# A graph network's attention loop: GpSimd forms half of the weighted rows, and three VectorE operations read one operand from PSUM

## What is computed

```
for r in range(8):
    h = x @ W[r]                                  # 3125 x 64
    e = leaky_relu((h @ a_src[r])[src] + (h @ a_dst[r])[dst])   # one number per edge
    e = where(edge_type == r or self loop, e, -inf)
    m = segment_max(e, dst)                       # per target node
    w = exp(e - m[dst]);  alpha = w / segment_sum(w, dst)[dst]
    out += segment_sum(alpha * h[src], dst) + bias[r]
```

## Time and profile before

| | before |
|---|---|
| runs, median | 3334.22 us |
| profiled execution: its own time | 3330.27 us |
| its span | 3328.6 us |
| attention loop, first gather to last | 147.5 to 1500.4 us of the span |
| VectorE busy over the span | 69% |
| VectorE busy, stretch 1076.14 to 1298.01 us | 215.07 of 221.87 us |
| GpSimd gathers | 976, mean 1070 ns, idle before them 321.2 us |

### The profile page before, as it was taken

How to read it: one execution, slowest core, us unless ns; L and a number is a source line. 1 busy time by engine, 2 the same in 40 slices (tenths; PEclk the granted TensorE clock), 3 DMA queues, 4 the chain that set the end, 5 groups by cost and what they waited for, 6 DMA issues and landing times. The chain is left out here.

```text
span 3328.6 us, 73440 instructions
## 1 busy us (share of the span) xinstructions
PE 2681.1 (81%) x15652; PEld 1854.9 (56%) x15653; DVE 2289.6 (69%) x7329; ACT 1362.5 (41%) x2946; POOL 1916.8 (58%) x1867
## 2 busy tenths in 40 slices
PE   7477777777777777777678988998888899999597
PEld 4246655655665565654233335555555566767495
DVE  7589999999999999997333336444444456655395
ACT  1155555555555555554000004444444444444101
POOL 0177777777777777770002004777777777777400
PEclk8556566666666666666878997888898899999798
DMA  4644444444444443441806342333333354554393
GB/s 138 129 124 126 134 125 125 125 125 143 120 130 121 137 131 101 112 119 49 252 1 210 90 128 53 86 82 82 82 81 82 81 136 131 140 140 125 129 328 117
DMA packets 584812, 405.42 MB, mean 122 GB/s; under 512 B 438561, under 2 KB 505428, under 8 KB 583702
## 3 DMA queue, kind: packets, MB, share of 16 engines
q10 hardware_dynamic: 86128, 184.53, 15.7%
q1 hardware_dynamic: 438968, 116.38, 15.6%
q0 software_dynamic: 59344, 100.63, 11.8%
HBM read 215.94 MB, written 210.09 MB: 128 GB/s over the span
## 5 line engine op out<-in xcount | busy, mean ns | idle before, releaser
L842 POOL DMA_INDIRECT at_hs<-table,at_rec_s x976 | 1044.7, 1070 | 321.2 <-issue 230.5
L2294 POOL DMA_INDIRECT edge_rows<-el_rows,el_idx x816 | 839.4, 1029 | 262.7 <-issue 236.2
L880 ACT CAST at_count_s<-near_ps 128x400 f16<-128x400 f32 x976 | 483.7, 496 | 628.2 <-PE near_ps L983 612.7
L983 PE MATMUL near_ps<-at_pair_hot,at_src_low_hot 128*128 128x425 f16 x976 | 470.8, 482 | 232.0 <-ACT at_count_s L880 213.4
L955 PEld LDWEIGHTS sums_ps<-at_hw,at_hit 128*128 128x128 f32 x1952 | 468.7, 331 | 32.8 <-issue 27.6
L955 PE MATMUL sums_ps<-at_hw,at_hit 128*128 128x66 f32 x1952 | 441.0, 407 | 8.4 <-DVE acc L1029 8.4
L983 PEld LDWEIGHTS near_ps<-at_pair_hot,at_src_low_hot 128*128 128x128 f16 x976 | 138.2, 142 | 337.6 <-ACT at_count_s L880 285.8
L1021 DVE TENSOR_SCALAR at_pair_hot<-iota_wide,at_rec_s 128x400 f16<-128x400 f16 x976 | 322.7, 333 | 0.7
L1029 DVE SCALAR_TENSOR_TENSOR acc<-acc,at_fade,sums_ps 128x66 f32 x976 | 266.7, 273 | 14.1 <-PE sums_ps L955 8.7
L2367 PE MATMUL el_h_ps<-w,el_h 128*128 128x128 f32 x1632 | 260.8, 308 | 0.0
L2535 DVE TENSOR_TENSOR el_idx<-el_place,el_aside 128x8 uint32<-128x8 f32 x102 | 17.4, 171 | 348.9 <-DMA edge_rows<-el_rows,el_idx 347.6
(11 more groups left out here) (432 smaller groups left out, 4563.6 us busy)
## 6 DMA issues: line engine op xcount, KB each, us to landing
slots<-at_count_s ACTq DMA_DIRECT2D x122, 850.0 KB
el_rec<-attr SPq DMA_DIRECT2D x816, 32.0 KB
chunk<-slots SPq DMA_DIRECT2D x256, 100.0 KB
attr<-in_edge_attr SPq DMA_DIRECT2D x16, 1472.0 KB
ts_rows<-edge_rows SPq DMA_DIRECT2D x74, 288.0 KB, 4.5
ts_rows<-edge_rows ACTq DMA_DIRECT2D x74, 288.0 KB, 4.6
chunk<-slots ACTq DMA_DIRECT2D x208, 100.0 KB
el_quad_rows<-edge_rows ACTq DMA_DIRECT2D x72, 288.0 KB
```

What stands on the lines that cost most here:

```text
L842: pool.indirect_dma_start(hs[:, s, u, :], None, k.table, bass.IndirectOffsetOnAxis(rec[:, s, u, 0:1].bitcast(U32), 0)).then_inc(gathered[s ...
L880: a.copy(count[:, (n.o + d) % 2, i, 0:AW], near[:, (n.o + d) % 2, 0:AW]).then_inc(count_ready, 1)
L983: pe.matmul(near[:, s, 0:SW], low_hot[:, s, i, :], pair_hot[:, s, i, :], start=False, stop=True, skip_group_check=(i > 0)).then_inc(near_r ...
L2294: pool.indirect_dma_start(k.edge_rows, bass.IndirectOffsetOnAxis(idx[:, o % RECS, 4 * h + u:4 * h + u + 1], 0), rows[:, j, u, :], None).th ...
```

## The change

GpSimd takes over half of the product `hw = hs * weight`. Its new function `low_hw` multiplies visits 0 to 3 of turn `n-5` after the fifth gather of turn `n`; VectorE keeps visits 4 to 7 where the whole product stood. TensorE's first half of `gather_sums` now waits for GpSimd's part (`low_hw_ready`), its second half for VectorE's (`hw_ready`). After the last gathers GpSimd goes on for five turns with products alone.

The numbers 0 to 127 are copied once into PSUM, and `miss` and `src_low_hot` read them there. The source scores of a turn are copied into PSUM at the head of VectorE's step (a new operation of eight numbers), and `far` reads them there. The two copies share one PSUM bank (`side`).

```diff
+        side = ps("side_ps", [P, CW])
+        iota_ps, score = side[:, 0:P], side[:, P:P + 2 * B].rearrange("p (s u) -> p s u", u=B)
...
+            def low_hw(n, d):
+                r, w = (n.o + d) % RING, (n.o + d) % 2
+                pool.wait_ge(gathered[r], (n.round(d) + 1) * (16 * B))
+                pool.sem_inc(passed, 1)
+                if n.after(2 - d):
+                    pool.wait_ge(sums_ready, n(1, d - 1))
+                    pool.sem_inc(passed, 1)
+                pool.wait_ge(weight_ready, n(1, d + 1))
+                pool.sem_inc(passed, 1)
+                nc.gpsimd.tensor_tensor(hw[:, w, 0:4], hs[:, r, 0:4], weight[:, w, 0:4].unsqueeze(2).to_broadcast([P, 4, TW]),
+                                        ALU.mult).then_inc(low_hw_ready, 1)
             def step(n):
                 if not n.has(0):
+                    if n.has(-5):
+                        low_hw(n, -5)
                     return
...
                     pool.wait_ge(hw_ready, n(1, 1 - RING))
+                    pool.sem_inc(passed, 1)
+                    pool.wait_ge(low_hw_ready, n(1, 1 - RING))
...
+                    if u == 4 and n.has(-5):
+                        low_hw(n, -5)
...
             turns(pool, 0, step)
+            for o in range(NB0 + 2, NB0 + 5):
+                step(Turn(o))
...
             def gather_sums(n, d, h):
+                if h == 1:
+                    pe.wait_ge(hw_ready, n(1, d + 1))
                 if h == 0:
-                    pe.wait_ge(hw_ready, n(1, d + 1))
+                    pe.wait_ge(low_hw_ready, n(1, d + 1))
...
+                if n.has(1):
+                    q = (n.o + 1) % RING
+                    dve.wait_ge(gathered[q], (n.round(1) + 1) * (16 * B))
+                    v.tensor_copy(score[:, w], hs[:, q, :, D + 1]).then_inc(score_copied, 1)
                 if here:
                     dve.wait_ge(masked_ready, n(2, 2))
...
-                    v.scalar_tensor_tensor(far[:, w], miss[:, w], -BIG, hs[:, q, :, D + 1:D + 2].to_broadcast([P, B, P]),
+                    v.scalar_tensor_tensor(far[:, w], miss[:, w], -BIG, score[:, w].unsqueeze(2).to_broadcast([P, B, P]),
...
-                    v.tensor_tensor(miss[:, m], key[:, m, 0].unsqueeze(2).to_broadcast([P, B, P]), k.iota_row[:].unsqueeze(1).to_broadcast([P, B, P]),
+                    v.tensor_tensor(miss[:, m], key[:, m, 0].unsqueeze(2).to_broadcast([P, B, P]), iota_ps.unsqueeze(1).to_broadcast([P, B, P]),
...
-                                    k.iota_low[:].unsqueeze(1).to_broadcast([P, B, P]), ALU.is_equal)
+                                    iota_ps.unsqueeze(1).to_broadcast([P, B, P]), ALU.is_equal)
...
-                        v.tensor_tensor(hw[:, w], hs[:, (n.o - 1) % RING],
-                                        weight[:, w].unsqueeze(2).to_broadcast([P, B, TW]), ALU.mult).then_inc(hw_ready, 1)
+                        v.tensor_tensor(hw[:, w, 4:B], hs[:, (n.o - 1) % RING, 4:B],
+                                        weight[:, w, 4:B].unsqueeze(2).to_broadcast([P, 4, TW]), ALU.mult).then_inc(hw_ready, 1)
```

More of the change, by code:

```diff
@@ L778, in attention @@
         deg_added, dst_copied = sem("deg_added"), sem("dst_copied")
+        low_hw_ready = sem("low_hw_ready")
         iota_ready, run_start, passed = sem("iota_ready"), sem("run_start"), sem("passed")
+        iota_copied, score_copied = sem("iota_copied"), sem("score_copied")
         rec_written = sem("records_written")
@@ L1041, in step @@
                 if n.has(1):
-                    q = (n.o + 1) % RING
-                    dve.wait_ge(gathered[q], (n.round(1) + 1) * (16 * B))
                     dve.wait_ge(key_step, n(2, 4))
+                    dve.wait_ge(score_copied, n(1, 2))
                     if n.after(1):
                         dve.wait_ge(hit_ready, n(2))
-                    v.scalar_tensor_tensor(far[:, w], miss[:, w], -BIG, hs[:, q, :, D + 1:D + 2].to_broadcast([P, B, P]),
+                    v.scalar_tensor_tensor(far[:, w], miss[:, w], -BIG, score[:, w].unsqueeze(2).to_broadcast([P, B, P]),
                                            ALU.mult, ALU.add).then_inc(far_ready, 1)
@@ L1138, in _ @@
             dve.wait_ge(iota_ready, 1)
+            v.tensor_copy(iota_ps, k.iota_row[:]).then_inc(iota_copied, 1)
+            dve.wait_ge(iota_copied, 1)
             turns(dve, -2, step)
```

## The result

The changed kernel takes 3359.9 us (median; 3358.06 to 3364.96) beside 3336.76 us for the kernel before on the same chip: a ratio of 1.0072, 95% interval 1.0056 to 1.0088. It is slower by about 24 us, within the range 3333 to 3385, 9 us over the forecast of 3351 and 2 us over 3358, the upper end that the prediction gives to the forecast itself.

A forecast was written before the change was run, and what follows sets the result against it. Prediction: TensorE and ScalarE, waiting for each other, bound the kernel. Profiled 3330.27 us + 12 (fill) + 5 (steady part) = 3347.3, with the median 3.95 us higher: 3351 us, its own range 3341 to 3358, overall 3333 to 3385.

The forecast's parts named there:

- The bound: In the loop, TensorE and ScalarE waiting for each other set the 11.09 us turn; VectorE has some 0.27 us to spare.
- What the change removes: Per turn, VectorE's product saves 0.28 us, GpSimd's shorter gathers about 0.96 us; PSUM inputs cost the wide operations nothing.
- The product: On GpSimd, 264 numbers take 0.83 us, ends 0.59 and 1.08, plus 0.1 of gap; GpSimd's turn becomes 10.9 us.
- The fill: At the loop's start, TensorE's first sum waits for 45 gathers, standing 15.2 us; net +12 us, from +10 to +16.
- The steady part: After the fill, GpSimd's product can hold VectorE, 10.64 to 11.19 us a turn: +5 us, from 0 to +11.
- The signs: Profile if right: first sum near 205 us, gathers 0.95 to 0.97, product 0.8 to 0.9, steady turns 11.0 to 11.2.
- VectorE held: Rival, chance 0.12: GpSimd's product holds VectorE each turn, 0.2 x 100 + 12 us, giving 3366 us.
- The change doesn't free GpSimd: Rival, chance 0.04: operations with PSUM inputs hold gathers as before, GpSimd needs 11.9 us a turn, giving 3443 us.

The follow-up runs named there:

- the PSUM operands alone: Changed kernel with the product of all eight visits back on VectorE, scores' copy and PSUM inputs kept: 3336.57 us beside 3336.23 for the kernel before, ratio 0.9995.
- the lighter VectorE: Changed kernel without VectorE's updates of visits 6 and 7 in each turn: 3347.18 us beside 3330.72 for the kernel before, ratio 1.0047.
- the small product: Changed kernel with GpSimd's product cut from 264 numbers to 4, waits and place kept: 3347.33 us beside 3336.23 for the kernel before, ratio 1.0034.
- own-half-first version: Changed kernel, GpSimd's product also waiting for VectorE's own half of that turn's product: 3353.66 us beside 3330.91 for the kernel before, ratio 1.0063.
- lag 5: GpSimd's product of turn n-5 as in the changed kernel, here also waiting for VectorE's own half: 3353.66 us, ratio 1.0063 to the kernel before.
- lag 4: Changed kernel with GpSimd's product of turn n-4 behind the fifth gather, here also waiting for VectorE's own half: 3338.9 us, ratio 1.0011 to the kernel before.
- the product alone: Changed kernel with GpSimd's product kept, but masks and scores read from SBUF as before: 3452.16 us beside 3336.23 for the kernel before, ratio 1.0333.

## Why the prediction was right, point by point, and where a size was off

- **The bound.** Right: the PSUM operands alone leave the time where it was, though they free GpSimd, and only work taken from ScalarE made the kernel faster. But "a turn takes 221.87 / 20 = 11.09 us" holds for the stretch that was read, at a granted clock of 0.65; 20 other turns of the same execution take 11.36 each at 0.61.
- **What the change removes.** Right: gathers of 963 ns (0.95 to 0.97 asked for); `miss` and `far` at 1.21 to 1.22. The 0.19 us that the Trainium skill ("VectorE: DVE Perf Modes", TRN2 errata) would put on three PSUM sources is not in these rows.
- **The product.** 0.64 us alone against the 0.83 that I took, near the low end of 0.59; the gaps are 0.02 before it and 0.16 behind it. GpSimd's turn is thus 8 x 0.96 + 7 x 0.30 + 0.02 + 0.64 + 0.16 = 10.6 us, not 10.9, and it waits at its gates instead of being the bound. The error was harmless.
- **The fill.** Right: first sum at 204.78 (205.2 forecast). Two kernels that keep it with no excess stand 11 and 16 us over before (intervals 6 to 16 and 10 to 21); +12 was forecast. The traces show it without the scatter of the times: the reduction of the tenth turn begins at 270.45 us before and at 282.17 after, 122.9 and 134.3 us behind the first gather, so the fill is 11.4 us.
- **The steady part.** Right in kind: "VectorE then needs 10.82 - 0.28 + 0.1 = 10.64 us" and 11.19 when held; the measured needs are 10.72 to 10.80 where the product holds little and 11.13 after. The size is not settled. The last step is "I take half of that for the 110 turns left: +5 us", with a range of 0 to 11. The medians put the loss at 8 us (1 to 16, over the lighter VectorE) or 13 (5 to 20, over the small product), a part of which may be the clock's; the excess, 14.1 and 8.9 us, counts too much. So +5 is at the low end or right. That it came this near is in part luck: the step treats the need as one number, but a tenth of the turns needs under 10.77 us and a tenth over 11.40; it treats the turn as one number, which the granted clock moves from 11.09 to 11.36; and it takes no account of VectorE's own half, which grows to 537 ns.
- **The signs.** The first sum, the gathers and the wide operations came out as forecast. The product was not 0.8 to 0.9 us. Turns were not 11.0 to 11.2 us but 11.20 to 11.34, by stretches of 19 or 20. And marks of 380 ns with TensorE's counts waiting for them are the sign that the prediction gave to its rival "VectorE held".
- **The range of the forecast.** Its ends, +10 to +16 and 0 to +11, with the 3.95 us that the forecast adds, give 3344 to 3361 us; the 3341 to 3358 that it states leaves the 3.95 out. The measured 3359.9 lies in the first and not in the second.
- **The rivals.** "The change doesn't free GpSimd" was priced at 3443 us; the product without the PSUM operands, which is that case, measured 3452. "VectorE is held each turn" named the mechanism of the steady loss too, and put 20 us on it.

The rule of the Trainium skill that bears on the hold ("SBUF — State Buffer", who interferes with whom) says that an operation with one SBUF input, outside the modes that use both ports, doesn't contend with GpSimd, and that of two that do the first to issue keeps the shared ports to its end. The first half agrees: updates, with one input in PSUM, stay at 0.27 us beside the product. Of the second half the traces show both sides: the mark at 624.32 keeps its 0.31 us and the product is the longer; the halves at 346.32 and 346.81 both grow, to 0.85 and 0.84 from 0.42 and 0.64, and at 403.78 it is the mark, the first to begin, that grows.

What stays open: how large the steady loss is, and how much of it is the clock's; whether after's excess differs from that of its own-half-first version, and whether the longer lead that the fill gives GpSimd is what moves the product late into the marks; the offsets agree with it (9.1 to 10.6 us with lag 5, 8.9 to 9.4 with lag 4, both with the wait on the own half), but no kernel changed the lead alone.

## What to carry to other kernels

An operation that is given to an engine with time to spare must be asked two things: behind how much queued work its first one stands (45 gathers here, 14 us once), and which operations of other engines grow beside it (marks from 333 to 380 ns here). Held operations cost nothing as long as the held engine's need stays under the turn. Count that turn by turn, and against the turn at the granted clock of that stretch: 0.65 and 0.60 gave different answers in one execution. And work moved off engines that are not the bound gains nothing: 0.22 us of a copy taken from ScalarE was worth more than some 0.86 us a turn freed on GpSimd (8 gathers of 963 instead of 1070 ns).

## What the runs showed of the hardware that was not expected

- A product of 264 numbers with two inputs takes 0.64 us on GpSimd, 0.22 us for 4 numbers, where the product of 16 in another stage takes 345 ns. With the masks and scores of VectorE back in SBUF (the product alone) the same 264 had a mean of 1.05 us.
- A mark, with one 16-bit tensor in SBUF and its result there, stretches beside the product to as much as 0.95 us, in the turn at 404 us although it began 0.18 us earlier; an update of 0.27 beside the same product does not.
- The gap behind a product ahead of the next gather is 0.16 us, half of the 0.30 between two gathers.
- The turn that TensorE and ScalarE set between them is 11.09 us at a mean granted TensorE clock of 0.65 and 11.36 at 0.61, in one execution of the kernel before.
